# Two output projections of a two-layer network: weights through four buffers, their low part made by VectorE, small loads on GpSimd's queue, and the router's matmuls and square sums inside layer 0's projection

## What is computed

```python
mod = (_silu(L0_c) @ L0_wmod).reshape(L0_c.shape[0], 6, 1, -1)
...
x = x + ga * _L0_attn_ref(h, ...)           # ends in o @ Wo
h = _layernorm(x, axis=-1) * (1 + cb) + sb
x = x + gb * _L0_ffn_ref(h, ...)            # 8 experts, top 2
mod = (_silu(L1_c) @ L1_wmod).reshape(L1_c.shape[0], 6, 1, -1)
...
x = x + ga * _L1_attn_ref(h, ...)           # ends in o @ Wo
h = _layernorm(x, axis=-1) * (1 + cb) + sb
x = x + gb * _L1_ffn_ref(h, ...)
```

```python
var = jnp.mean(jnp.square(x), axis=-1, keepdims=True)
router_input = x * jax.lax.rsqrt(var + 1e-06)
router_input = router_input * root_size * router_scale
logits = jnp.einsum('gsd,de->gse', router_input, router_logits)
probs = jax.nn.softmax(logits32, axis=-1)
_, choices = jax.lax.approx_max_k(logits32, k=k)
```

## Time and profile before

| | |
|---|---|
| Median of 3 runs | 2972.35 us (2969.6 to 2975.65) |
| The profiled execution's own time | 2968.18 us |
| Its span on the core | 2966.5 us |
| PE busy | 85% of the span |
| DVE, ACT, POOL busy | 60%, 42%, 33% |
| Mean granted PE clock | 0.912 of full speed |
| HBM traffic | 134 GB/s over the span |

### The profile page before, as it was taken

How to read it: one execution, slowest core, us unless ns; L and a number is a source line. 1 busy time by engine, 2 the same in 40 slices (tenths; PEclk the granted TensorE clock), 3 DMA queues, 4 the chain that set the end, 5 groups by cost and what they waited for, 6 DMA issues and landing times. The chain is left out here.

```text
span 2966.5 us, 32511 instructions
## 1 busy us (share of the span) xinstructions
PE 2514.0 (85%) x9340; PEld 1654.1 (56%) x9340; DVE 1779.3 (60%) x2639; ACT 1233.9 (42%) x2446; POOL 968.6 (33%) x999
## 2 busy tenths in 40 slices
PE   7999859999999996873899998258998875699989
PEld 6788624444444443670688887144454324588767
DVE  4310239999999994543455554449999994411143
ACT  3232037777777784231455554452223113211121
POOL 0111023333333332536000000318999993111010
PEclk9999969999999996876899999679999997799979
DMA  5253356666656652853777773634444445210032
GB/s 181 85 174 113 101 133 155 160 162 160 164 154 160 167 145 68 289 208 141 243 230 231 229 231 116 208 106 161 167 169 172 169 147 172 63 29 21 6 101 64
DMA packets 306643, 441.61 MB, mean 149 GB/s; under 512 B 50024, under 2 KB 132984, under 8 KB 306528
## 3 DMA queue, kind: packets, MB, share of 16 engines
q1 hardware_dynamic: 272368, 389.39, 43.4%
q10 hardware_dynamic: 28720, 33.10, 3.1%
q0 software_dynamic: 5440, 17.70, 1.7%
HBM read 303.85 MB, written 94.32 MB: 134 GB/s over the span
## 5 line engine op out<-in xcount | busy, mean ns | idle before, releaser
L1000 ACT ACTIVATE attn_probs<-attn_ps_score,attn_nmax 128x512 f32<-128x512 f32 x512 | 342.6, 673 | 4.9 <-DVE attn_nmax L1076 3.4
L2422 PE MATMUL scan_ps_o<-scan_qs,scan_sel 128*128 128x512 f32 x512 | 267.4, 637 | 74.0 <-DVE scan_qs L2366 68.3
L2384 DVE TENSOR_TENSOR_SCAN scan_st<-scan_ps_dec,scan_kv 128x512 f32<-128x512 f32 x256 | 307.3, 1216 | 13.3 <-POOL scan_kv L2336 12.9
L913 PE MATMUL attn_ps_score<-attn_KK,attn_S 128*128 128x512 f32 x512 | 273.2, 534 | 40.2 <-ACT attn_probs L1000 37.4
L913 PEld LDWEIGHTS attn_ps_score<-attn_KK,attn_S 128*128 128x128 f32 x512 | 99.2, 194 | 221.3 <-ACT attn_probs L1000 197.1
L2422 PEld LDWEIGHTS scan_ps_o<-scan_qs,scan_sel 128*128 128x128 f32 x512 | 88.8, 194 | 228.1 <-DVE scan_qs L2366 146.5
L841 POOL TENSOR_TENSOR attn_masked<-attn_spread,attn_q 128x512 f32<-128x512 f32 x96 | 123.2, 1286 | 278.6 <-DMA attn_spread<-rows 170.8
L1090 DVE SCALAR_TENSOR_TENSOR attn_mixed<-attn_probs,attn_cf,attn_mixed 128x512 f32<-128x512 f32 x256 | 199.1, 778 | 9.1
L1065 DVE TENSOR_REDUCE attn_raw<-attn_ps_score 128x2 f32<-128x1024 f32 x128 | 156.0, 1219 | 23.6 <-PE attn_ps_score L915 23.4
L2336 POOL TENSOR_TENSOR scan_kv<-scan_vb,gla_gk 128x512 f32<-128x512 f32 x128 | 161.3, 1274 | 17.4 <-DMA scan_vb<-gv 7.3
L1010 ACT ACTIVATE attn_probs<-attn_probs,attn_cf 128x512 f32<-128x512 f32 x128 | 92.4, 722 | 171.1 <-DVE attn_cf L1081 171.1
(11 more groups left out here) (431 smaller groups left out, 6386.2 us busy)
## 6 DMA issues: line engine op xcount, KB each, us to landing
scan_vb<-gv SPq DMA_DIRECT2D x256, 256.0 KB
moe_raw<-in_L_ffn_gating SPq DMA_DIRECT2D x92, 512.0 KB, 4.5
attn_spread<-rows SPq DMA_DIRECT2D x64, 384.0 KB, 8.7
moe_raw<-in_L_ffn_linear SPq DMA_DIRECT2D x46, 512.0 KB
attn_S<-attn_X SPq DMA_DIRECT2D x64, 256.0 KB, 4.3
attn_S<-attn_Y SPq DMA_DIRECT2D x128, 128.0 KB, 4.3
rows_x<-out_zeros SPq DMA_DIRECT2D x23, 512.0 KB, 7.6
moe_xb<-rows_x SPq DMA_DIRECT2D x23, 512.0 KB, 6.2
```

Source lines behind the costliest of these rows:

```text
L913: nc.tensor.matmul(ps_score[n][:, j, :], S[p][:, 2 * n + j, cols], KK[p][:, :], start=True, stop=False)
L1000: nc.scalar.activation(probs[b][:, at_j, :], ps_score[n][:, j, :], ACT.Exp, bias=nmax[b][:, at_j:at_j + 1], accum_out=Z[b][:, at_j:at_j + ...
L2384: V.tensor_tensor_scan(st[r][:, :], ps_dec[n % 2][:, :], kv[r][:, :], 0.0, ALU.mult, ALU.add).then_inc(st_ready, 1)
L2422: nc.tensor.matmul(ps_o[w][:, :], sel[:, P - GPH - GPH * d:2 * P - GPH - GPH * d], qs[i % RING][:, :], start=(d == 0), stop=(d == HALF - 1 ...
```

## The change

In both projections: four weight buffers in place of two (`RAWS`), the weights' low part made by DVE in place of POOL, the eight `modT` loads issued from POOL's queue at the stage's start in place of SP's, and ACT's wait for them moved from ahead of `high(1)` into the first `take`. In layer 0 only: the router's weights and scale are loaded here, scaled by DVE, and the logits of sequence `b` are made on PE after tiles 7, 11 and 15 and at the end (`logits`), copied out by ACT (`router`), and the square sums of `h` are made by ACT (`squares`); for this the projection has three banks in place of four, since the logits take one, `hT` holds two sequences in place of four, and the clearing of `rows_x` starts at tile 2. The experts' stage loses the logits, the square sums and their loads. Cut to its core:

```diff
@@ -1152,7 +1152,8 @@
         KC, NT = Wo.shape[0] // P, B * TT
-        raw_w = [m.sb(f"raw_w{p}", [P, D]) for p in two]
+        RAWS, BANKS = 4, 4 if h is None else 3
+        raw_w = [m.sb(f"raw_w{i}", [P, D]) for i in range(RAWS)]
...
-        hT = s["hT"]
+        if h is None:
+            hT = s["hT"]
+        else:
+            hT = m.sb("hT", [P, 2, DC, T])
+            Wr, Ws, sq = m.sb("Wr", [P, DC, E]), m.sb("Ws", [P, DC, 1]), m.sb("sq", [P, D])
+            ps_logit = m.ps("ps_logit")
+            r_in, scale_in, r_ready, logit_done, logit_taken, squared = (m.sem(n) for n in (
+                "r_in", "scale_in", "r_ready", "logit_done", "logit_taken", "squared"))
+        kept = lambda b: b % 2 if h is not None else b
...
@@ -1188,11 +1200,13 @@
         @block.sync
         def _(sp):
             for j in range(KC):
-                if j >= 2:
-                    sp.wait_ge(wlo_ready, j - 1)
-                sp.dma_start(raw_w[j % 2][:, :], Wo[j * P:(j + 1) * P, :]).then_inc(w_in[j % 2], 16)
+                if j >= RAWS:
+                    sp.wait_ge(wlo_ready, j - RAWS + 1)
+                sp.dma_start(raw_w[j % RAWS][:, :], Wo[j * P:(j + 1) * P, :]).then_inc(w_in[j % RAWS], 16)
                 if j < 2:
                     sp.dma_start(o_raw[j][:, :, :], ov[j]).then_inc(o_in[j], 16)
+            if h is not None:
...
-                if n == 0:
-                    for q in two:
-                        for c in range(DC):
-                            at = (kind + 1 + q) * D + c * P
-                            sp.dma_start(modT[:, q, c, :], s["mod"][layer, :, at:at + P].rearrange("b p -> p b"),
-                                         allow_slow_non_contiguous=True).then_inc(mod_in, 16)
...
-                    if n == 0:
+                    if n == FILL_FROM:
                         sp.wait_ge(zeros_ready, 1)
-                    for k in range(n * many // NT, (n + 1) * many // NT):
+                    for k in range((n - FILL_FROM) * many // (NT - FILL_FROM) if n >= FILL_FROM else 0,
+                                   (n + 1 - FILL_FROM) * many // (NT - FILL_FROM) if n >= FILL_FROM else 0):
...
@@ -1234,6 +1243,14 @@
         def _(pool):
             identity(nc, nc.gpsimd, ident, const_ready)
             nc.gpsimd.memset(eps[:, :], EPS).then_inc(const_ready, 1)
+            for q in two:
+                for c in range(DC):
+                    at = (kind + 1 + q) * D + c * P
+                    pool.dma_start(modT[:, q, c, :], s["mod"][layer, :, at:at + P].rearrange("b p -> p b"),
+                                   allow_slow_non_contiguous=True).then_inc(mod_in, 16)
+            if h is not None:
+                pool.dma_start(Ws[:, :, 0], a["L0_ffn_router_scale"].rearrange("(c p) -> p c", p=P),
+                               allow_slow_non_contiguous=True).then_inc(scale_in, 16)
...
             low(0)
-            for j in range(KC):
-                pool.wait_ge(whi_ready, j + 1)
-                nc.gpsimd.tensor_tensor(W[1][:, j, :], raw_w[j % 2][:, :], W[0][:, j, :].bitcast(F32), ALU.subtract
-                                        ).then_inc(wlo_ready, 1)
...
+            def logits(b):
+
+                if b == 0:
+                    pe.wait_ge(r_ready, 1)
+                pe.wait_ge(hT_ready, DC * (b + 1))
+                if b:
+                    pe.wait_ge(logit_taken, b)
+                for t in range(TT):
+                    for c in range(DC):
+                        last = nc.tensor.matmul(ps_logit[:, t * E:(t + 1) * E], hT[:, kept(b), c, t * P:(t + 1) * P], Wr[:, c, :],
+                                                start=(c == 0), stop=(c == DC - 1))
+                last.then_inc(logit_done, 1)
...
-                if n >= 4:
-                    pe.wait_ge(gated, n - 3)
+                if n >= BANKS:
...
                 if n % TT == 1 and n > TT:
                     turn(n // TT - 1)
+                if h is not None and n % TT == TT - 1 and n > TT:
+                    logits(n // TT - 1)
             turn(B - 1)
+            if h is not None:
+                logits(B - 1)
 
         @block.scalar
...
             def take(b):
 
+                if b == 0:
+                    act.wait_ge(mod_in, 16 * 2 * DC)
+                if h is not None and b >= 2:
+                    act.wait_ge(logit_done, b - 1)
...
+            def router(b):
+
+                act.wait_ge(logit_done, b + 1)
+                nc.scalar.copy(s["logit"][:, TT * b:TT * (b + 1), :].rearrange("p n e -> p (n e)"), ps_logit[:, 0:TT * E]
+                               ).then_inc(logit_taken, 1)
+
+            def squares(b):
+                for t in range(TT):
+                    n = TT * b + t
+                    act.wait_ge(shifted, n + 1)
+                    if n:
+                        act.wait_ge(squared, n)
+                    nc.scalar.activation(sq[:, :], h[:, n, :], ACT.Square, accum_out=s["ssq"][:, n:n + 1]).then_inc(squared, 1)
+
...
             for j in range(KC):
-                act.wait_ge(w_in[j % 2], 16 * (j // 2 + 1))
-                nc.scalar.copy(W[0][:, j, :], raw_w[j % 2][:, :]).then_inc(whi_ready, 1)
+                act.wait_ge(w_in[j % RAWS], 16 * (j // RAWS + 1))
+                nc.scalar.copy(W[0][:, j, :], raw_w[j % RAWS][:, :]).then_inc(whi_ready, 1)
             act.wait_ge(const_ready, 3)
-            act.wait_ge(mod_in, 16 * 2 * DC)
             for n in range(NT):
...
+                if h is not None and b >= 2 and t == 1:
+                    router(b - 2)
+                    squares(b - 2)
             root(B - 1)
             store(B - 1)
             take(B - 1)
+            if h is not None:
+                for b in (B - 2, B - 1):
+                    router(b)
+                    squares(b)
             for p in two:
...
+            for j in range(KC):
+                dve.wait_ge(whi_ready, j + 1)
+                V.tensor_tensor(W[1][:, j, :], raw_w[j % RAWS][:, :], W[0][:, j, :].bitcast(F32), ALU.subtract
+                                ).then_inc(wlo_ready, 1)
+            if h is not None:
+                dve.wait_ge(r_in, 16)
+                dve.wait_ge(scale_in, 16)
+                for c in range(DC):
+                    last = V.tensor_scalar(Wr[:, c, :], Wr[:, c, :], Ws[:, c, :], float(D) ** -0.5, ALU.mult, ALU.mult)
+                last.then_inc(r_ready, 1)
...
@@ -1492,16 +1554,12 @@
...
         def _(sp):
-            sp.dma_start(Wr[:, :, :], a["L0_ffn_router_logits"].rearrange("(c p) e -> p c e", p=P)).then_inc(c_in, 16)
-            sp.dma_start(Ws[:, :, 0], a["L0_ffn_router_scale"].rearrange("(c p) -> p c", p=P),
-                         allow_slow_non_contiguous=True).then_inc(c_in, 16)
             sp.dma_start(pes[:, :], a["L0_ffn_per_expert_scale"].partition_broadcast(P)).then_inc(c_in, 16)
             wmod = a["L1_wmod"].rearrange("(c p) m -> p c m", p=P)
             for k in range(6):
                 sp.dma_start(mod_w[k][:, :, :], wmod[:, :, k * D:(k + 1) * D]).then_inc(mod_in[k], 16)
             sp.wait_ge(experts_ready, 1)
             sp.wait_ge(mod_done, 6)
-            sp.wait_ge(ssq_done, NT)
...
         def _(pe):
-            pe.wait_ge(cw_ready, 1)
-            for n in range(NT):
-                for c in range(DC):
-                    last = nc.tensor.matmul(ps_logit[:, n * E:(n + 1) * E], hT[:, n // TT, c, n % TT * P:(n % TT + 1) * P],
-                                            Wr[:, c, :], start=(c == 0), stop=(c == DC - 1))
-            last.then_inc(r_done, 1)
...
         def _(act):
-            for n in range(NT):
-                if n:
-                    act.wait_ge(ssq_done, n)
-                nc.scalar.activation(sq[:, :], h[:, n, :], ACT.Square, accum_out=ssq[:, n:n + 1]).then_inc(ssq_done, 1)
...
-            dve.wait_ge(c_in, 48)
-            for c in range(DC):
-                last = V.tensor_scalar(Wr[:, c, :], Wr[:, c, :], Ws[:, c, :], float(D) ** -0.5, ALU.mult, ALU.mult)
-            last.then_inc(cw_ready, 1)
             by_e = lambda z: z[:, :].unsqueeze(2).to_broadcast([P, NT, E])
             by_n = lambda z: z[:, :].unsqueeze(1).to_broadcast([P, NT, E])
 
-            dve.wait_ge(ssq_done, NT)
-            V.tensor_scalar(ms[:, :], ssq[:, :], 1.0 / D, 1e-6, ALU.mult, ALU.add).then_inc(std_in, 1)
+            V.tensor_scalar(ms[:, :], s["ssq"][:, :], 1.0 / D, 1e-6, ALU.mult, ALU.add).then_inc(std_in, 1)
...
-            dve.wait_ge(r_done, 1)
-            lgp = ps_logit[:, 0:NT * E].rearrange("p (n e) -> p n e", e=E)
-            ch.link(V.tensor_tensor(lg[:, :, :], lgp, by_e(r1), ALU.mult))
+            ch.link(V.tensor_tensor(lg[:, :, :], s["logit"][:, :, :], by_e(r1), ALU.mult))
...
-            keep(ctx, "hT", [P, B, DC, T])
```

32 lines of the change are left out of this document (19 added, 13 removed).

## The result

The changed kernel took 2961.86 us (median of 6 runs, 2960.99 to 2963.52), the kernel before 2972.86 us (6 runs, 2967.61 to 2975.65). The ratio is 0.9966, with a 95% interval of 0.9955 to 0.9976: 11.0 us less, where I had forecast 35.2 less. The direction was right and the time, 2962, lies outside my range of 2921 to 2960.

What follows compares the result with a forecast made beforehand. PE, busy 85%, was taken as the bound, with gains from its idle or hideable stretches. The terms -16.7 + 7.7 + 7.6 - 26.6 - 7.2 = -35.2 us gave 2933.0, forecast as 2937 us against the runs' median; range 2921 to 2960.

Steps and rivals of the forecast that it cites:

- Start of layer 0's projection: Layer 0's projection: PE starts later behind POOL's nine issues, but tile 1 ends at 1191.0 instead of 1207.68, gaining 16.7 us.
- by then everything else is there: Layer 0's projection: when PE starts, weights come through four buffers and DVE splits a chunk in about 0.69 us.
- the third rival: Both projections' starts: full DMA engines let modT delay o's tiles, so only issue time is saved; 2945 us, 8%.
- Logits of sequences 0 and 1: Layer 0's projection, behind tiles 7 and 11: 3.84 us each, straight on PE's path, +7.7 us.
- The second rival: Layer 0's projection: the logits cool PE to a lower clock, +10.9 us, 2948 us; chance 12%.
- End of the stage: Layer 0's projection after tile 15: sequence 3's logits, copy and squares make 20.9 us against 13.25, +7.6 us.
- the forecast's list of signs: Signs expected in the profile, among them the stage after layer 0's projection starting within 5 us of 1299.
- Experts' stage: Experts' start: logits leave, modulation starts 6.4 us in, waits only for its first load, ends 29.0 us in; -26.6 us.
- Layer 1's projection: Layer 1's projection: only the first part of the change applies; tile 3 ends at 2483.1 instead of 2490.33, -7.2 us.
- The rival on the slower side: Both projections' starts: POOL's issues become the bound; above 3.4 us each the change loses, 2983 us at 4 us; 7%.

Runs made afterwards that it cites:

- the padded kernel: Changed kernel with 448 unused bytes a partition behind its two kept tensors, so that together they take 1024: 2935.79 us, ratio 0.9874 to the kernel before.
- the two halves alone: Kernel before with only the edits at both projections' start: 2947.95 us; changed kernel with those edits undone and 448 bytes of padding: 2960.64 us.
- the three repaired ones: Changed kernel with its two kept tensors allocated after layer 0's attention, 2939.36 us; with 448 padding bytes, 2935.79; with all tensors of 512 bytes or more aligned, 2934.04.
- The 512-byte move: Kernel before with one unused tensor of 512 bytes a partition in front, moving all later tensors by 512 bytes: 2975.39 us, ratio 0.9996.
- the kernel with only the attention's inputs moved: Kernel before with 64 bytes in front of the attention's inputs and 448 behind, so only these start 64 past a multiple of 512: 2992.86 us, ratio 1.0073.
- the move: Kernel before with only the two small kept tensors added, unused, moving later tensors by 576 bytes: 3000.07 us, ratio 1.0097.

## Why the forecast was right and wrong

**The step that failed is one that is missing.** The sum took every stage outside the two projections and the experts' start for unchanged. It priced the instructions and waits that the diff moves, and had no term for the two kept tensors at its end. Their true price is +27.5 us by themselves, in a stage that the forecast never looked at. With it, -35.2 + 27.5 = -7.7, and 11.0 was measured. In the padded kernel, where that price is gone, the change gives 39.0 us (its interval is 32 to 43); the two halves alone gave 24.6 and 10.8, together 35.4 against the forecast's 35.2. The agreement to 0.2 us is partly luck, with runs that spread over 10 to 28 us.

**Start of layer 0's projection**, forecast -16.7 at tile 1's end: -17.3 there, and -15.3 at tile 2's. The mechanism was right and two sizes off, in opposite ways. A modT issue on POOL costs 0.76 us and not 1.3, so PE starts 11.5 us in and not 15.7 (1177.7 - 1161.96). This by itself would have given 4.9 us more. But "by then everything else is there" was wrong: the last weights arrived at 1207.5, 17 us in, and the third tile of o kept ACT for 8.03 us. The DMA engines' share was 0.99, 0.80 and 1.05 in that time, which is the third rival's mechanism in part; how much of it is modT's pieces and how much the loads that now come earlier, no run separates. 0.76 us is nearer to the 0.55 that I had set beside the rule of the Trainium skill (DMA: Bandwidth & Descriptors, "Anatomy of one DMA — SWDGE (gpsimd) path") than to my 1.3.

**Logits of sequences 0 and 1**, forecast +7.7: +8.8 between tiles 2 and 15 (77.7 us before, 86.5 after). Each took 3.63 to 3.94 us, at the high clock as forecast. The second rival came true in part, much smaller than its 10.9 us: in the changed kernel the clock fell behind each. In the padded one it stayed high, and tile 8 came after 8.59 us in place of 10.17:

```profile
1226.34 0.67 DVE L1464 TENSOR_TENSOR out_y<-out_bank,out_g 128x512 f32<-128x512 f32 x1
...
1234.93 0.69 DVE L1464 TENSOR_TENSOR out_y<-out_bank,out_g 128x512 f32<-128x512 f32 x1 [0.55 <-issue]
```

So a dip costs 1.6 us, two of them 3.2. Between tiles 2 and 15 the padded kernel took 83.3 us, 5.6 more than before and not the 7.3 that its two logits last; why it is less was not looked into. So the 8.8 for 7.7 is a term too large by 2 and a missing one of 3, and their near agreement is luck. Four of the five profiles with the logits there have the dips; what decides is open.

**End of the stage**, forecast +7.6: +7.9 (21.2 us behind tile 15's end, before 13.25), with the last logits at 6.96 us where 6.9 was forecast. The three terms so far leave the stage 1.4 us shorter, which puts the next one at 1302.7 and not at the 1299 of the forecast's list of signs. It came out 1.4 us longer, 143.5 us for 142.1.

**Experts' stage**, forecast -26.6: -26.35 (40.2 us for 66.6). The modulation started 5.96 us in, forecast 6.4, and only its first load was waited for.

**Layer 1's projection**, forecast -7.2: -10.4 at tile 3 by the two profiles. The cheaper issue is worth 8 x 0.54 = 4.3 us here, of which 3.2 came by this pair. The profile before is the slowest of its kind in this stretch, though. Over this whole stretch the eight other kernels with the old start took 111.9 to 113.9 us, where the profile before had 115.15, and the five with the new one 104.0 to 105.8: on their means the gain is 7.8, close to the forecast.

**Between the scatter and layer 1's projection** the changed kernel lost 5.7 us against the profile before, and two of the three repaired ones 3.2 and 4.6. The 512-byte move, with every remainder kept, also shows 3.5, and the kernel with only the attention's inputs moved, in which nothing of this stretch differs, shows 7.1. How much of the 5.7 us is the change's stays open.

**The rival on the slower side**, POOL's issues as the bound, is out at 0.76 us. The result could have fallen on its side by another way: by the measured prices, without the router edits the start edits and the move would about cancel, -24.6 + 27.5.
